# Second graph layer's score stage: TensorE runs 22 of its 25 tile groups in an engine loop of 11 turns

## The chip, the cores and the metric

The kernel runs on one core of one Trainium2 chip. The metric is the device time of one execution in microseconds (us), lower is better. "TensorE" is PE in the profile (its weight loads are PEld), "VectorE" is DVE, "ScalarE" is ACT, "GpSimd" is POOL, and the queue that only issues DMAs is SP.

## The reference, cut to what matters

The model is four graph layers, each followed by a feed-forward layer, on 384 nodes of 512 features with 12288 edges. The change lies in the third graph layer by position, called L2 in the code (the second layer of the kind that scatters messages along sorted edges, counting from L0). What it computes:

```python
h_src = h[src]                                   # rows of h = x @ W.T, 8 heads of 64
e_src = einsum('ehd,hd->eh', h_src, a_src)
e_dst = einsum('ehd,hd->eh', h[dst], a_dst)
e = leaky_relu(e_src + e_dst, 0.2) * (1 + et_emb[edge_type]) * edge_weight[:, None]
e_max = zeros((n, h_)).at[dst].max(e)
e = exp(e - e_max[dst]);  e_sum = zeros((n, h_)).at[dst].add(e)
alpha = e / (e_sum[dst] + 1e-10)
out = zeros(...).at[dst].add(h_src * alpha[:, :, None])
```

The score stage is the sum `e_src + e_dst` for every edge and head. Everything from `leaky_relu` on needs it.

## The kernel before

Edges lie sorted by destination in 98 tiles of 128 (`TT2 = 98`), worked in groups of four (`GT = 4`), so 25 groups (`GG`), the last of two tiles. One group passes through four steps on three engines:

- **Key rows** (TensorE, `key_row`, L2481): for each of two keys (source node, destination node within its chunk of 128), four matmuls spread a column of key values, broadcast as weights, over a bank of PSUM. Two banks, jobs `l2b{g}0` and `l2b{g}1`, eight matmuls of 128 columns in 16-bit float.
- **Copy** (ScalarE, L2551): each bank goes to SBUF as `key_rows`, 128x512.
- **Compare** (VectorE, L2659): four comparisons with the node number give `node_hot`, one-hot matrices, and the semaphore `nodes_ready` counts the group.
- **Score** (TensorE, L2496 to L2505): per tile four matmuls of 24 columns into one bank, job `l2e{g}`. Three have fixed operands, the fourth reads `dst_parts` at a place that comes from a register (`four[j]`). The registers are loaded from a list in SBUF, four tiles at once, by `chunks_of` (L678). VectorE then sums the bank to `w_edge` (`score`, L2650), one group behind its comparisons.

TensorE's program is written out: key rows of group g+2, then the wait for `nodes_ready` of group g, then the scores of group g. PSUM has eight banks, handed out in turn by `Banks.open` (L54), so a bank comes back after 8 jobs, that is after 2.7 groups. Each bank has two semaphores, "full" (counted up by TensorE's last matmul of the job) and "free" (counted up by its reader). `Banks.loop` (L66) exists for TensorE loops elsewhere in the kernel, and waits inside such a loop compare with a value that depends on the turn's number.

At the same time GpSimd gathers rows of `tab_h` with indirect DMAs (`pool_scatter_rows`, L633): one DMA for each of the 98 tiles, in series of six, with a wait for their landing between. There are 39 places for rows, so DMA 39 waits until the scatter stage has used the first. Ahead of the 13th and the 20th DMA (`POOLED_SCORES`) GpSimd waits for the scores of groups 0 to 8 and 9 to 15, and scales them with four operations each (L2587 to L2590). The rest is scaled by VectorE at L2669 and L2672, then the maxima are formed (L2677 to L2700), and the scatter stage begins (`pe_scatter_rows`, L694): for each tile one matmul of 128x512 float32 on the gathered row and one of 24 columns.

The first graph layer has a TensorE loop of 13 turns of 8 tiles (L958), all of whose large matmuls take an operand at a place from a register. It serves as a measure of such operands.

Of the kernel before, what the change touches and what calls it, by code (L numbers as in the profile page):

```python
# [162 lines left out]
def gnn_ffn_program(nc, A, out):  # L163
    ctx = ExitStack()
    with ctx:
# [511 lines left out]

        def chunks_of(T):  # L678
            _, some = nc.values_load_multi_w_load_instructions(
                chunk2_i[0:1, T:min(T + 4, TT2)], engines=[mybir.EngineType.PE], min_val=0, max_val=NT - 1,  # L680
                skip_runtime_bounds_check_because="a sum of two comparisons is 0, 1 or 2")
            return some

# [1751 lines left out]
        POOLED_SCORES = {12: (0, 9), 19: (9, 16)}  # L2435
        SCORED_LATE = GT * 16

        w_here = {}

        def along(v):  # L2440
# [14 lines left out]
        @on("pe")  # L2455
        def _(pe, o):
            pe.wait_ge(tiles_loaded, 16)
            b = banks.open(pe, "l2n")
            nc.tensor.transpose(b[0:TT2, 0:P], dst2, ident[:])
            for s_, lane in enumerate((0, P - 1)):  # L2460
                last = mm(b[0:H8, P + s_ * TT2:P + (s_ + 1) * TT2], ident[:, lane:lane + 1].broadcast_to([P, H8]), dst2, True, True)
            last.then_inc(banks.full_of("l2n"), 1)
            wT = ring.get(pe, 0)
            w_here["L2"] = 16 * ring.got[0]
            ends = banks.open(pe, "l2a_")
            for t in range(NT):
                for k in ((0,), (1, 2), ())[t]:
                    pe_turn_block(pe, "l2x", xn, k, 3 * NT)
                if t == 0:
                    pe.wait_ge(cols_ready, 1)  # L2470
                banks.drained(pe, f"l2x{t}")
                b = banks.open(pe, f"l2r{t}")
                for c in range(KC):
                    own = xT[:, c, t * P:(t + 1) * P]
                    last = mm(b, own, wT[:, c, :], c == 0, c == KC - 1)
                    if c == KC - 1:
                        last.then_inc(banks.full_of(f"l2r{t}"), 1)
                    last = mm(ends[:, t * 2 * H8:(t + 1) * 2 * H8], own, fold[:, c, :], c == 0, c == KC - 1)
            last.then_inc(banks.full_of("l2a_"), 1)

            def key_row(g):  # L2481
                for f in range(2):
                    b = banks.open(pe, f"l2b{g}{f}")
                    for j in range(min(GT, TT2 - GT * g)):
                        last = mm(b[:, j * P:(j + 1) * P], key_cols[:, f, GT * g + j:GT * g + j + 1].broadcast_to([P, P]), ident_h,
                                  True, True)
                    last.then_inc(banks.full_of(f"l2b{g}{f}"), 1)

            pe.wait_ge(cols_ready, 2)
            key_row(0)  # L2490
            key_row(1)
            pe.wait_ge(step_ready, 6)
            for g in range(GG):
                if g + 2 < GG:
                    key_row(g + 2)
                pe.wait_ge(nodes_ready, g + 1)  # L2496
                b = banks.open(pe, f"l2e{g}")
                four = chunks_of(GT * g)
                for j in range(min(GT, TT2 - GT * g)):
                    o = b[:, j * 3 * H8:(j + 1) * 3 * H8]  # L2500
                    for c in range(NT):
                        mm(o, node_hot[:, g % 2, c, j * P:(j + 1) * P], parts[:, 0, c, :, :].rearrange("p k h -> p (k h)"),
                           c == 0, False)
                    last = mm(o, node_hot[:, g % 2, NT, j * P:(j + 1) * P], dst_parts[:, bass.ds(four[j] * 3 * H8, 3 * H8)], False, True)
                last.then_inc(banks.full_of(f"l2e{g}"), 1)  # L2505

            pe.wait_ge(lanes_ready, 1)
            banks.at = SUMS + 1
            for k in range(2):
                b = banks.open(pe, f"l2t{k}")  # L2510
                for h in range(HH):
                    last = nc.tensor.transpose(b[0:TT2, h * P:(h + 1) * P], w_edge[:, :, HH * k + h], ident[:])
                last.then_inc(banks.full_of(f"l2t{k}"), 1)
            pe_clear_sums(pe, "l2")
            banks.at = SUMS + 3
            pe.wait_ge(lanes_ready, 2)
            b = banks.open(pe, "l2m")
            mm(b[0:H8, 0:TT2], weight[:, :, 0], ident[0:TT2, 0:TT2], True, True)
            mm(b[0:H8, TT2:2 * TT2], top[:, :, P - 1], ident[0:TT2, 0:TT2], True, True).then_inc(banks.full_of("l2m"), 1)
            pe.wait_ge(lanes_ready, 3)  # L2520
            b = banks.open(pe, "l2w")
            for s_ in range(2):
                last = mm(b[0:TT2, s_ * H8:(s_ + 1) * H8], lane_fwd[:, :, s_], ident[0:H8, 0:H8], True, True)
            last.then_inc(banks.full_of("l2w"), 1)
            banks.at = SUMS + 3
            for k in range(2):
                pe.wait_ge(lanes_ready, 4 + k)
                b = banks.open(pe, f"l2v{k}")
                for h in range(HH):
                    last = nc.tensor.transpose(b[:, h * TT2:(h + 1) * TT2], weight[:, HH * k + h, :], ident[0:TT2, 0:TT2])  # L2530
                last.then_inc(banks.full_of(f"l2v{k}"), 1)
            pe_scatter_rows(pe, "l2")

        @on("act")
        def _(act, o):

            act_row_std(act, ROW_L2, 0)
            act_turned_block(act, "l2x", xT, 0)
            for t in range(1, NT):
                act_row_std(act, ROW_L2 + t, t)  # L2540
            for t in range(1, NT):
                act_turned_block(act, "l2x", xT, t)
            for t in range(NT):
                act_copy(act, f"l2r{t}", hrows[:, t, :])
            for g in range(GG):
                if g >= 2:
                    act.wait_ge(nodes_ready, g - 1)
                for f in range(2):
                    b = banks.filled(act, f"l2b{g}{f}")
                    n = P * min(GT, TT2 - GT * g)  # L2550
                    nc.scalar.activation(key_rows[:, g % 2, f, 0:n], b[:, 0:n], ACT.Copy).then_inc(banks.free_of(f"l2b{g}{f}"), 1)  # L2551
            act_hot_half(act, 0)
            for k in range(2):
                b = banks.filled(act, f"l2v{k}")
                nc.scalar.activation(w_tile[:, HH * k:HH * k + HH, :].rearrange("p h t -> p (h t)"), b[:, 0:HH * TT2],
                                     ACT.Exp).then_inc(banks.free_of(f"l2v{k}"), 1)
            for i in range(1, TT2 // RB):
                act_hot_half(act, i)
            banks.drained(act, "l2s")
            for t in range(1, NT):  # L2560
                b = banks.filled(act, f"l2a{t}")
                for h in range(H8):
                    last = nc.scalar.activation(xn2[:, t, h * HD:(h + 1) * HD], b[:, h * HD:(h + 1) * HD], ACT.Identity,
                                                scale=gate[:, 4, t * H8 + h:t * H8 + h + 1])
                last.then_inc(banks.free_of(f"l2a{t}"), 1)
                if t == 1:
                    act_row_std(act, ROW_F2, 0)
            act_row_std(act, ROW_F2 + 1, 0)
            for t in range(1, NT):
                act_row_std(act, ROW_F2 + 2 * t, t)  # L2570
                act_turned_block(act, "f2x", xT, t - 1)
                act_row_std(act, ROW_F2 + 2 * t + 1, t)
            act_turned_block(act, "f2x", xT, NT - 1)

        @on("pool")
        def _(pool, op):
# [3 lines left out]
            def between(T):  # L2580
                if T not in POOLED_SCORES:
                    return
                g0, g1 = POOLED_SCORES[T]
                banks.all_drained(pool, [f"l2e{g}" for g in range(g0, g1)])
                own = slice(GT * g0, GT * g1)
                small = sel8[:, own, :]
                op.link(nc.gpsimd.tensor_scalar(small, w_edge[:, own, :], 0.0, 0.2, ALU.min, ALU.mult))  # L2587
# [48 lines left out]
        def _(dve, od):  # L2636
# [8 lines left out]
            nc.vector.memset(gate[:, 15, 5:6], 0.0).then_inc(step_ready, 1)  # L2645

            def score(g):
                b = banks.filled(dve, f"l2e{g}")
                n = min(GT, TT2 - GT * g)
                nc.vector.tensor_reduce(w_edge[:, GT * g:GT * g + n, :],  # L2650
                                        b[:, 0:n * 3 * H8].rearrange("p (t k h) -> p t h k", t=n, k=3), AX,
                                        ALU.add).then_inc(banks.free_of(f"l2e{g}"), 1)

            for g in range(GG):
                n = P * min(GT, TT2 - GT * g)
                for f in range(2):
                    banks.drained(dve, f"l2b{g}{f}")
                    for c in range(NT) if f == 0 else (0,):
                        last = nc.vector.tensor_scalar(node_hot[:, g % 2, c + NT * f, 0:n], key_rows[:, g % 2, f, 0:n],  # L2659
                                                       node_id[:, c:c + 1], None, ALU.is_equal)  # L2660
# [1 line left out]
                if g >= 1:  # L2662
                    score(g - 1)
            score(GG - 1)
            banks.all_drained(dve, [f"l2e{g}" for g in range(GG)])

            late = slice(SCORED_LATE, TT2)
            dve.wait_ge(factor_ready, 1)
# [624 lines left out]
```

## Time and profile before

| | us |
|---|---|
| median of 3 runs | 1792.34 (1790.09 to 1795.05) |
| profiled execution | 1795.19 |
| its span, first to last instruction | 1793.4 |
| PE busy | 1601.0 (89%) |
| DVE busy | 881.6 (49%) |
| ACT busy | 501.5 (28%) |
| POOL busy | 642.0 (36%) |

The profile's times are counted from the start of the span. Waits that the trace can't connect with an instruction's end are marked "remote": the semaphore moved, but no instruction that counts it up ended shortly before. "issue" is time in which an engine waited for nothing that the profile shows. PEclk is the share of full clock that TensorE was granted. Register operations, branches and waits of the sequencers are not among the rows.

### The profile page before, as it was taken

The numbers are of one execution on the slowest core, as the hardware profiler recorded it, in microseconds if no ns is written. First come the engines' busy times: TensorE is split into PE (matmuls) and PEld (weight loads), VectorE is DVE, ScalarE is ACT, GpSimd is POOL, SyncE is SP. The second block draws the span as 40 slices with busy tenths as digits, with TensorE's granted clock in tenths as the row PEclk, the third lists the DMA queues.
The fourth block names the chain that finished last, engine by engine and source line by source line (L and its number), as shares of the span: only waits on it lengthen the run. The fifth ranks groups of instructions, "written<-read, shape, count | busy, mean of one in ns | idle before, by whom it ended". The sixth has DMA issues, their size and how long they took to land. (4 is left out here: it accounts for less than half of the span.)

```text
span 1793.4 us, 22802 instructions
## 1 busy us (share of the span) xinstructions
PE 1601.0 (89%) x6910; PEld 888.4 (50%) x6940; DVE 881.6 (49%) x2161; ACT 501.5 (28%) x1586; POOL 642.0 (36%) x756
## 2 busy tenths in 40 slices
PE   6989999998697999999996877589799999999798
PEld 3534444446444645555553645334344555555555
DVE  8878888878644343344354154598623101111322
ACT  1134444447431413223231124311200111111234
POOL 5868787873332333333341713556300000000000
PEclk9989999999698999999997887589799999999899
DMA  8030101005413223122316744445326121220020
GB/s 313 2 102 25 60 25 60 25 8 133 124 48 127 78 82 90 57 81 63 94 42 135 255 138 140 138 133 160 118 71 216 51 91 52 99 67 16 9 62 18
DMA packets 119611, 161.71 MB, mean 90 GB/s; under 512 B 49497, under 2 KB 61721, under 8 KB 119154
## 3 DMA queue, kind: packets, MB, share of 16 engines
q1 hardware_dynamic: 93056, 115.43, 20.6%
q0 software_dynamic: 18592, 29.91, 6.1%
q10 hardware_dynamic: 7890, 15.44, 2.6%
q8 instruction: 41, 0.67, 0.2%
q14 instruction: 32, 0.26, 0.1%
HBM read 145.26 MB, written 15.47 MB: 90 GB/s over the span
## 5 line engine op out<-in xcount | busy, mean ns | idle before, releaser
L373 PE MATMUL psum<-arena 128*128 128x384 f32 (+9 forms) x1804 | 319.8, 333 | 33.0 <-issue 13.3
L373 PE MATMUL psum<-arena,ring 128*128 (+1 forms) x1478 | 323.2, 364 | 9.0 <-issue 6.3
L373 PE MATMUL psum<-xT,ring 128*128 128x384 f32 x928 | 317.5, 503 | 10.4 <-ACT ring L3118 4.5
L373 PEld LDWEIGHTS psum<-arena 128*128 128x128 f32 (+5 forms) x1804 | 197.3, 155 | 162.8 <-issue 88.3
L373 PE MATMUL psum<-ring,arena 128*128 128x512 f32 (+1 forms) x570 | 261.9, 607 | 8.6 <-DVE ring L663 3.9
L373 PE MATMUL psum<-ring,xT 128*128 128x512 f32 x552 | 253.9, 613 | 2.1 <-DMA bc<-in_wide 0.8
L373 PEld LDWEIGHTS psum<-xT,ring 128*128 128x128 f32 x928 | 181.5, 197 | 139.9 <-issue 28.3
L373 PEld LDWEIGHTS psum<-arena,ring 128*128 128x128 bf16 (+1 forms) x1504 | 139.7, 115 | 130.3 <-issue 29.0
L1071 ACT ACTIVATE ring<-ring 128x128 f32<-128x128 f32 x416 | 123.3, 297 | 173.6 <-DVE ring L1357 164.6
L373 PEld LDWEIGHTS psum<-ring,xT 128*128 128x128 f32 x552 | 106.0, 197 | 125.4 <-issue 121.6
L373 PEld LDWEIGHTS psum<-ring,arena 128*128 128x128 f32 (+1 forms) x570 | 99.7, 188 | 131.3 <-issue 130.2
L851 POOL DMA_INDIRECT tab_bucketed<-rec,pos x96 | 95.7, 997 | 190.0 <-DMA tab_bucketed<-rec,pos 182.4
L2144 POOL DMA_INDIRECT tab_sorted<-rec,pos x104 | 100.0, 962 | 173.2 <-DMA tab_sorted<-rec,pos 151.1
L1357 DVE SCALAR_TENSOR_TENSOR ring<-psum,wa 128x1024 f32<-128x1024 f32 x104 | 127.3, 1224 | 61.4 <-PE psum L373 60.5
L1165 POOL TENSOR_SCALAR arena<-iota,arena 128x128 bf16<-128x128 f32 x200 | 121.6, 616 | 16.8 <-DVE xT L1371 13.9
L1177 POOL DMA_INDIRECT tab_w<-xT,pair x104 | 109.8, 1056 | 48.8 <-DMA tab_w<-xT,pair 31.9
L408 ACT ACTIVATE arena<-psum 128x384 f32<-128x384 f32 (+1 forms) x130 | 61.9, 498 | 182.8 <-PE psum L373 157.6
L482 ACT ACTIVATE std<-mv,eps_col 128x1 f32<-128x1 f32 x57 | 16.8, 294 | 220.9 <-DVE mv L465 217.9
L1071 ACT ACTIVATION_READ_ACCUMULATOR ring<-ring 128x1 f32 x416 | 77.5, 186 | 0.0
L624 POOL DMA_INDIRECT ring<-tab_h,sd_t x61 | 62.6, 1026 | 37.1 <-issue 13.3
L2071 DVE TENSOR_TENSOR xn<-xn,psum 128x512 f32<-128x512 f32 x24 | 16.5, 687 | 118.7 <-PE psum L373 118.5
L1365 DVE TENSOR_REDUCE mask_dst<-ring 128x4 f32<-128x512 f32 x104 | 70.2, 675 | 0.0
(478 smaller groups left out, 1667.3 us busy)
## 6 DMA issues: line engine op xcount, KB each, us to landing
ring<-in_L_ffn_w SPq DMA_DIRECT2D x22, 1024.0 KB, 6.8
ring<-in_L_gnn_m_w SPq DMA_DIRECT2D x8, 1024.0 KB, 6.0
ring<-in_L_ffn_expert_weights SPq DMA_DIRECT2D x8, 1024.0 KB
ring<-tab_key ACTq DMA_DIRECT2D x24, 256.0 KB
ring<-in_L_gnn_Wv SPq DMA_DIRECT2D x5, 1024.0 KB, 5.1
tab_w<-xn SPq DMA_DIRECT2D x6, 768.0 KB, 14.7
ring<-in_L_gnn_Ww SPq DMA_DIRECT2D x4, 1024.0 KB
ring<-in_L_gnn_wq SPq DMA_DIRECT2D x4, 1024.0 KB
```

Source lines behind the costliest of these rows:

```text
L373: return nc.tensor.matmul(o, a, b, start=start, stop=stop)
L408: nc.scalar.activation(dst, b[:, 0:w], ACT.Copy).then_inc(banks.free_of(name), 1)
L482: nc.scalar.activation(std[:, t:t + 1], mv[:, t, 1:2], ACT.Sqrt, bias=eps_col[:, 0:1]).then_inc(row_std, 1)
L624: return nc.gpsimd.indirect_dma_start(o, None, table, bass.IndirectOffsetOnAxis(ap=column.bitcast(U32), axis=0), **more)
L851: nc.gpsimd.indirect_dma_start(tab_bucketed, bass.IndirectOffsetOnAxis(ap=pos[:, q:q + 1].bitcast(U32), axis=0), rec[:, q, :], None).then_ ...
L1071: last = nc.scalar.activation(prod2[:, b % 2, h, :], prod2[:, b % 2, h, :], ACT.Copy, accum_out=w_sum[:, b, h:h + 1])
L1165: last = nc.gpsimd.tensor_scalar(edge_is[:, j, k, s_, :], iota[:, 0:P], key_rq[:, s_, T:T + 1], None, ALU.is_equal)
L1177: nc.gpsimd.indirect_dma_start(tab_w, bass.IndirectOffsetOnAxis(ap=pair[:, q:q + 1].bitcast(U32), axis=0), w_edge0[:, q, :], None).then_in ...
L1357: V.scalar_tensor_tensor(out=prod2[:, b % 2], in0=z_bank[:, b % 2], scalar=0.0, in1=wa_all, op0=ALU.max, op1=ALU.mult).then_inc(z_free, 1)
L1365: V.tensor_reduce(w_sum[:, b, 0:H8 // 2], prod2[:, b % 2, 0:H8 // 2, :], AX, ALU.add).then_inc(halves_summed, 1)
L2071: V.tensor_tensor(xn2[:, t, :], xn2[:, t, :], b, ALU.add).then_inc(banks.free_of(f"{tag}{t}"), 1)
L2144: nc.gpsimd.indirect_dma_start(tab_sorted, bass.IndirectOffsetOnAxis(ap=pos2[:, q:q + 1].bitcast(U32), axis=0), rec[:, q, :], None).then_i ...
```

## The change

Key rows and scores of a group become functions that take either fixed numbers or a place that depends on the loop's register. Groups 0 to 21 run in an engine loop of TensorE, 11 turns of two groups; groups 22 to 24 stay written out. In the loop the column of key values, the place in the list of chunks, and the values that the waits compare with all come from the turn's register. The loop uses six banks, the same ones in every turn, so a bank comes back after two groups. The other engines stay written out, and their waits name the same banks by the new jobs. GpSimd and VectorE wait for the last two or five groups' banks rather than for one job of each bank.

```diff
         def chunks_of(T):
             _, some = nc.values_load_multi_w_load_instructions(
-                chunk2_i[0:1, T:min(T + 4, TT2)], engines=[mybir.EngineType.PE], min_val=0, max_val=NT - 1,
+                chunk2_i[0:1, slice(T, min(T + 4, TT2)) if isinstance(T, int) else bass.ds(T, 4)], engines=[mybir.EngineType.PE], min_val=0, max_val=NT - 1,
...
+        TURNS = (GG - 3) // 2
+        def key_job(g, f):
+            return (f"l2b{g % 2}{f}_", (g - 2) // 2) if 2 <= g < 2 * TURNS + 2 else (f"l2b{g}{f}", None)
+
+        def score_job(g):
+            return (f"l2e{g % 2}_", g // 2) if g < 2 * TURNS else (f"l2e{g}", None)
...
-            def key_row(g):
+            def key_row(g, tiles=GT, at=None, i=None):
                 for f in range(2):
+                    job = key_job(g, f)[0]
+                    b = banks.open(pe, job, i)
+                    for j in range(tiles):
+                        col = key_cols[:, f, GT * g + j:GT * g + j + 1] if at is None else key_cols[:, f, bass.ds(at + j, 1)]
+                        last = mm(b[:, j * P:(j + 1) * P], col.broadcast_to([P, P]), ident_h, True, True)
+                    last.then_inc(banks.full_of(job), 1)
+
+            def scored(g, tiles=GT, at=None, i=None):
+                job = score_job(g)[0]
+                pe.wait_ge(nodes_ready, g + 1 if i is None else 2 * i + g + 1)
+                b = banks.open(pe, job, i)
+                four = chunks_of(GT * g if at is None else at)
+                for j in range(tiles):
                     o = b[:, j * 3 * H8:(j + 1) * 3 * H8]
                     for c in range(NT):
                         mm(o, node_hot[:, g % 2, c, j * P:(j + 1) * P], parts[:, 0, c, :, :].rearrange("p k h -> p (k h)"),
                            c == 0, False)
                     last = mm(o, node_hot[:, g % 2, NT, j * P:(j + 1) * P], dst_parts[:, bass.ds(four[j] * 3 * H8, 3 * H8)], False, True)
-                last.then_inc(banks.full_of(f"l2e{g}"), 1)
+                last.then_inc(banks.full_of(job), 1)
+
+            pe.wait_ge(cols_ready, 2)
+            key_row(0)
+            key_row(1)
+            pe.wait_ge(step_ready, 6)
+            with banks.loop(TURNS, 6, first=banks.at), pe.Fori(0, TURNS) as i:
+                for h in range(2):
+                    key_row(2 + h, at=2 * GT * i + GT * (2 + h), i=i)
+                    scored(h, at=2 * GT * i + GT * h, i=i)
+            for g in range(2 * TURNS, GG):
+                if g + 2 < GG:
+                    key_row(g + 2, min(GT, TT2 - GT * (g + 2)))
+                scored(g, min(GT, TT2 - GT * g))
...
-                banks.all_drained(pool, [f"l2e{g}" for g in range(g0, g1)])
+                for g in (g1 - 2, g1 - 1):
+                    banks.drained(pool, *score_job(g))
...
-            banks.all_drained(dve, [f"l2e{g}" for g in range(GG)])
+            for g in range(2 * TURNS - 2, GG):
+                banks.drained(dve, *score_job(g))
```

## Rows read from the trace of the kernel before

**Rows 1.** Page: busy us of each engine (share of the span) xinstructions.

```profile
PE 1601.0 (89%) x6910; PEld 888.4 (50%) x6940; DVE 881.6 (49%) x2161; ACT 501.5 (28%) x1586; POOL 642.0 (36%) x756
```

**Rows 2.** Chain that ended last, in order of time: start us, us, what.

```profile
1154.37 0.46 DVE arena L2669
...
1173.43 0.51 ACT arena L2555
1174.02 0.70 DVE arena L663
1174.96 54.40 PE psum L373 x159
...
1272.27 4.14 DMA ring<-tab_h,sd_t
```

**Rows 3.** Waits, 1092.3 to 1154: waiter <- waited for: us, times, longest.

```profile
DVE arena L2650 <- remote: 24.2, 6, 5.3
ACT arena L2551 <- remote: 18.4, 7, 4.6
PE psum L373 <- DVE arena L2659: 12.6, 11, 3.1
```

**Rows 4.** Timeline of VectorE: start us, us, engine line op, count, [idle before <-releaser].

```profile
1093.22 0.26 DVE L2650 TENSOR_REDUCE arena<-psum 128x32 f32<-128x96 f32 x1 [0.72 <-PE psum L373]
1097.20 1.13 DVE L2659 TENSOR_SCALAR arena<-arena,node_id 128x512 bf16<-128x512 f16 x4
...
1127.14 0.26 DVE L2650 TENSOR_REDUCE arena<-psum 128x32 f32<-128x96 f32 x1 [5.32 <-remote]
1128.36 0.25 DVE L2650 TENSOR_REDUCE arena<-psum 128x32 f32<-128x96 f32 x1
1129.69 0.26 DVE L2650 TENSOR_REDUCE arena<-psum 128x32 f32<-128x96 f32 x1
...
1145.08 0.26 DVE L2650 TENSOR_REDUCE arena<-psum 128x32 f32<-128x96 f32 x1
1149.25 0.26 DVE L2650 TENSOR_REDUCE arena<-psum 128x32 f32<-128x96 f32 x1 [2.73 <-remote]
1153.61 0.37 DVE L2650 TENSOR_REDUCE arena<-psum 128x32 f32<-128x96 f32 x2 [3.33 <-remote]
```

**Rows 5.** Timeline, 1109 to 1116, TensorE, ScalarE and VectorE.

```profile
1111.07 0.50 PE L373 MATMUL psum<-arena 128*128 128x24 bf16 x5 [0.51 <-DVE arena L2659]
1111.40 0.60 ACT L2551 ACTIVATE arena<-psum 128x512 f16<-128x512 f32 x1 [2.98 <-remote]
1112.78 0.18 PE L373 MATMUL psum<-arena 128*128 128x24 bf16 x1 [1.21 <-issue]
1113.50 0.18 PE L373 MATMUL psum<-arena 128*128 128x24 bf16 x1 [0.54 <-issue]
1115.77 0.26 DVE L2650 TENSOR_REDUCE arena<-psum 128x32 f32<-128x96 f32 x1 [5.13 <-remote]
```

**Rows 6.** Stretches: us, PE, PEld, DVE, ACT, POOL busy (x), PEclk, DMA share, GB/s.

```profile
1130.00:1135.00 5.00, 4.63 (x79) 4.30 (x78) 4.94 (x16) 3.77 (x7) 3.77 (x5) 0.51 0.19 56
1138.00:1142.50 4.50, 1.98 (x20) 1.12 (x20) 0.00 (x0) 0.64 (x2) 2.79 (x3) 0.53 0.71 195
1096.40:1096.83 0.43, 0.43 (x18) 0.43 (x16) 0.00 (x0) 0.00 (x0) 0.43 (x1) 0.50 0.97 338
198.53:221.44 22.91, 22.25 (x135) 10.93 (x136) 18.48 (x52) 10.22 (x65) 16.15 (x22) 1.00 0.28 93
```

**Rows 7.** Timeline of TensorE: three runs of matmuls in the stage.

```profile
1090.46 0.62 PE L373 MATMUL psum<-arena 128*128 128x128 f16 x8 [0.43 <-DVE gate L2645]
...
1098.76 0.40 PE L373 MATMUL psum<-arena 128*128 128x24 bf16 x7 [1.09 <-DVE arena L2659]
...
1146.94 0.84 PE L373 MATMUL psum<-arena 128*128 128x24 bf16 x16 [0.67 <-DVE arena L2659]
```

**Rows 8.** First layer's loop, one such matmul per tile: min/median/max ns, first and last start.

```profile
L373 PE MATMUL psum<-ones_b,arena x104: 167/167/211, 106.8 to 403.2; 128*128 128x1 bf16 x104
```

**Rows 9.** DMA queues, 1087 to 1155: packets, MB, share of 16 engines.

```profile
q0 software_dynamic: 2400, 7.87, 38.9%
q1 hardware_dynamic: 1472, 2.90, 12.4%
q8 instruction: 5, 0.08, 0.4%
```

**Rows 10.** Waits of GpSimd, 1155 to 1178, and its timeline around its first scaling.

```profile
POOL arena L624 <- PE psum L373: 7.6, 1, 7.6
...
1113.32 0.94 POOL L624 DMA_INDIRECT ring<-tab_h,sd_t  x1 [0.30 <-issue]
1114.29 1.23 POOL L2587 TENSOR_SCALAR arena<-arena 128x288 f32<-128x288 f32 x1
```

More of the change, by code:

```diff
@@ L2436, in gnn_ffn_program @@
         SCORED_LATE = GT * 16
+        TURNS = (GG - 3) // 2
+        assert 2 * TURNS + 3 == GG
+        def key_job(g, f):
+            return (f"l2b{g % 2}{f}_", (g - 2) // 2) if 2 <= g < 2 * TURNS + 2 else (f"l2b{g}{f}", None)
+        def score_job(g):
+            return (f"l2e{g % 2}_", g // 2) if g < 2 * TURNS else (f"l2e{g}", None)
         w_here = {}
@@ L2479, in _ @@
             last.then_inc(banks.full_of("l2a_"), 1)
-            def key_row(g):
+            def key_row(g, tiles=GT, at=None, i=None):
                 for f in range(2):
[L2483 to L2499, printed above, removed]
+                    job = key_job(g, f)[0]
[10 more added lines that the diff above has]
+                for j in range(tiles):
                     o = b[:, j * 3 * H8:(j + 1) * 3 * H8]
@@ L2548, in _ @@
                 for f in range(2):
-                    b = banks.filled(act, f"l2b{g}{f}")
+                    b = banks.filled(act, *key_job(g, f))
                     n = P * min(GT, TT2 - GT * g)
-                    nc.scalar.activation(key_rows[:, g % 2, f, 0:n], b[:, 0:n], ACT.Copy).then_inc(banks.free_of(f"l2b{g}{f}"), 1)
+                    nc.scalar.activation(key_rows[:, g % 2, f, 0:n], b[:, 0:n], ACT.Copy).then_inc(
+                        banks.free_of(key_job(g, f)[0]), 1)
             act_hot_half(act, 0)
@@ L2647, in score @@
             def score(g):
-                b = banks.filled(dve, f"l2e{g}")
+                b = banks.filled(dve, *score_job(g))
                 n = min(GT, TT2 - GT * g)
@@ L2651, in score @@
                                         b[:, 0:n * 3 * H8].rearrange("p (t k h) -> p t h k", t=n, k=3), AX,
-                                        ALU.add).then_inc(banks.free_of(f"l2e{g}"), 1)
+                                        ALU.add).then_inc(banks.free_of(score_job(g)[0]), 1)
             for g in range(GG):
@@ L2656, in _ @@
                 for f in range(2):
-                    banks.drained(dve, f"l2b{g}{f}")
+                    banks.drained(dve, *key_job(g, f))
                     for c in range(NT) if f == 0 else (0,):
```

## The prediction

> **What bounds the kernel now.** I read the page first: TensorE is busy 89% of the span [rows 1], but that is an average, and the question is what ends the score stage and what its end moves. The chain of waits after the stage runs without a gap from VectorE's L2669 at 1154.37 through the maxima to the scatter stage, which starts at 1174.02 and in which TensorE holds the chain for 54.4 us at a stretch [rows 2]. So a score stage that ends later moves all that follows by the same time. An earlier end is worth less: GpSimd's DMA 39 waited 7.6 us for the scatter stage [rows 10], and the chain ends the scatter stage on the landing of the last gathered row, 4.14 us [rows 2]. Once the gain passes about 8 us, the gathers set the pace and the rest of it is lost.
>
> Next the stage itself, by waits and timeline. VectorE sums group 0 at 1093.22 and group 21 at 1145.08: 21 steps in 51.86 us, 2.47 us a group; the last three groups follow by 1153.98 [rows 4]. But the three steps from 1127.14 to 1129.69 are 1.22 and 1.33 us [rows 4]. The difference is in six waits of VectorE marked "remote", 24.2 us together, and seven of ScalarE, 18.4 us [rows 3]. In such a wait TensorE's matmuls had long been recorded, yet their semaphores did not move. At 1111.07 five matmuls go out, then one at 1112.78 and one at 1113.50, and the sum that VectorE waits for starts only at 1115.77 [rows 5]. From 1130 to 1135 TensorE does 79 matmuls; from 1138 to 1142.5 it does 20, while the DMA share goes from 0.19 to 0.71 [rows 6]. These **stops** fall into the series of gathers, which are the stage's largest traffic (2400 packets, 7.87 MB) [rows 9]. What they are the trace does not say. What matters here is that the stage is paced by two things, the clear pace of about 1.3 us a group, and the stops.
>
> **The change part by part.** What is taken away: TensorE's code for 20 of 22 groups need not be loaded. The stage loads five blocks of code [rows 9]. I cost this at nothing, and the rival below tells what it would be worth if that is wrong. Matmuls, copies, comparisons and sums are the same in number and size. The transfers that GpSimd and SP issue are the same too, and SP is not moved past anything.
>
> What is added is work of TensorE's sequencer, and no row shows such work by itself, so I bound it.
>
> (a) *An operand from a register.* A group's 16 score matmuls, four of them with one, take 0.84 us less the last one's own 0.18, so 0.66 us [rows 7], where TensorE with work in hand does 18 in 0.43 us, 0.024 us each [rows 6]. Four such operands so cost between (0.66 - 16 x 0.024)/4 = 0.07 us, if the plain matmuls count fully, and 0.66/4 = 0.165 us, if they hide. The first layer's loop gives the same upper end: 104 tiles from 106.8 to 403.2 us are 2.88 us a tile [rows 8] with 17 such matmuls, 0.17 us each, but there TensorE is busy for 22.25 of 22.91 us [rows 6], so it hides some. I take 0.12, the middle, as both rows bear on it.
>
> (b) *Key rows.* Eight matmuls with fixed operands take 0.62 us less 0.22 for the last, 0.057 us each [rows 7]. With an operand from a register each they take 8 x 0.12 = 0.96 us of the sequencer (0.56 to 1.36).
>
> (c) *Start of the scores.* From the end of the comparisons at 1097.20 + 1.13 = 1098.33 [rows 4] to the first score matmul at 1098.76 [rows 7] are 0.43 us: the wait, and the load of the four registers. The place in the list is now computed, one more of (a): 0.12.
>
> (d) *Waits with a value from the register.* Four a group (two key banks, `nodes_ready`, one score bank). No row has one alone; between nothing and the price of an address, so 0 to 0.66 a group. I take 0.24, half of four times 0.12, since in (a) the address is the nearest thing.
>
> (e) *The turn's end.* The first layer's loop idles 0.66 us in a whole turn [rows 6], so at most 0.66, at least nothing, per turn of two groups here; I take 0.15 a group.
>
> A group in the loop: 0.43 + 0.12 + 0.66 + 0.96 + 0.24 + 0.15 = **2.56 us**; with all the low ends 0.43 + 0.07 + 0.66 + 0.56 = 1.72, with all the high ones 0.43 + 0.17 + 0.66 + 1.36 + 0.66 + 0.33 = 3.61. VectorE's 1.3 us no longer paces the stage in clear stretches; TensorE's sequencer does. The edit is not hidden: the cover it has is the 1.3 us pace and the waits of TensorE for the comparisons, 12.6 us over the stage [rows 3], and 22 x (2.56 - 1.3) = 28 us is more than that. What is queued behind TensorE's waits are its own next key rows, and ScalarE and VectorE wait for those.
>
> Six banks rather than eight: a key bank is wanted back after two groups. ScalarE's copy of it was made before the comparisons that TensorE has by then waited for, so this costs nothing at 2.56 us a group.
>
> Without any stop 21 steps take 21 x 2.56 = 53.8 us, against 51.86 now: **+1.9 us**. Of the stops now, 24.2 - 2.73 - 3.33 = 18.1 us lie in these 21 steps [rows 3, 4]. How much stays is the hard step. If TensorE does nothing in a stop, all stays: +1.9 + 18.1 = +20. If the stops come only of the dense stream of matmuls, none stays: +1.9. What speaks for between: in a stop TensorE still did 20 matmuls in 4.5 us [rows 6], and a slower stream takes longer to run into one. At 24 matmuls per 2.56 us it would want 42 in that time. I take that 60% stays, 0.6 x 18.1 = 10.9, so **+13 us**. The last three groups are as before.
>
> GpSimd waits for group 8 ahead of its 13th DMA. Now it needn't (1113.32 + 0.94, then L2587 at 1114.29 [rows 10]); then group 8 comes some 5 us later and the gathers slip with it, also ahead of the 20th. DMA 39 waited 7.6 us, and the scatter stage slips by 13 us itself, so this stays covered; without that cover it would add its own 5 to 10 us.
>
> The profiled execution took 1795.19, so profiled 1808; the median of the runs is 2.85 below it, so **1792.3 + 13 = 1805 us**.
>
> **What the Trainium skill says against this change.** In the first layer's loop, whose turn holds 135 matmuls and 136 weight loads, TensorE is idle for 0.66 us in a whole turn [rows 6]. The Trainium skill, "Runtime: NRT & Kernel Launch", section "Instruction fetch mechanics", says that code is streamed in blocks of 256 instructions, mostly hidden, and that a taken branch to a block outside the two-block window stalls until it is fetched. By it a turn's end could stall here, if the turn lies across a block's edge; by the row it does not, for a longer turn, and the sum takes (e) from the row. The same section's "mostly hidden" is also against the second rival below.
>
> **The rivals.**
>
> *The stops go away altogether.* For it: the first layer's loop has a thinner stream (135 matmuls in 22.91 us, 6 per us against 16 per us from 1130 to 1135 [rows 6]) and is almost gapless with other indirect DMAs beside it. The loop here would have 9 per us. Against: TensorE was thin in the stops too. It gives +2, less up to 6 if the three last groups lose their stops (2.73 + 3.33 [rows 4]): 1788 to 1798, likeliest 1794, so "same".
>
> *The stops are code loading, and it is faster.* For it: five blocks [rows 9] and about five stops. Against: matmuls already recorded got their semaphores late [rows 5], which code that is not there yet can't do. If so, all 18.1 us of stops go, and with operands at the low end (1.72 us a group, 36 us for 21 steps) the stage ends 16 us earlier; at the middle price it is no gain, so this decides only below 2.2 us a group. Of the 16, some 8 pass the gathers: 1784.
>
> *The stops take the added instructions too.* If a stop holds back every instruction of the sequencer, address work included, then there are a third more of them and the stops grow: 24 instead of 18.1 us, and with 2.7 us a group rather than 2.56, since the waits of (d) then cost nearer their high end, 57 + 24 - 52 = +29: 1821.
>
> *The change doesn't do what it says,* as when the stage's end is set elsewhere: 1792.
>
> **How the numbers follow.** My forecast, slower by 6 to 20 us: 0.47. The added instructions in the stops: 0.15. Stops gone: 0.22 (of it 0.17 same, 0.03 slower, 0.02 faster). Code loading: 0.13 (0.11 faster, 0.02 same). No effect: 0.03, same. About 0.3%, 5.4 us, is what a measurement here can tell from no change. Slower 0.65, same 0.22, faster 0.13. The range runs from 1788, the low end of the gone stops, to 1823, above the forecast with whole stops (+20) and the third rival's 1821; outside are the code loading case and the high ends of all prices.
>
> **What would show it.** Right: VectorE's steps from sum to sum in clear stretches go from 1.3 to about 2.6 us; "remote" waits of VectorE fall to about 10 us; VectorE's wait for TensorE at L2650 rises well over the few us it has now; L2669 starts at about 1167. Blocks of code in the stage fall from five to two or so. Operands too dear or cheap: clear steps of 3 or 2 us. Stops gone: no "remote" wait left. Code loading: the stops end with the blocks. The forecast is wrong in sign if clear steps are below 2.2 us and the stops are gone.

## The result, and the profile after

The changed kernel takes 1794.37 us (median of 20 runs, 1791.01 to 1798.76) against 1790.67 us before (20 runs, 1788.29 to 1795.05): ratio 1.0020, 95% interval 1.0013 to 1.0027. So it is slower, by 3.7 us, which is less than the 0.3% that I had called "same". I forecast 1805, +13. The profiled execution took 1795.85 us, with a span of 1794.0, against 1795.19 and 1793.4.

Page after: busy us of each engine, then the queue that loads code (41 packets in the whole execution before).

```profile
PE 1609.5 (90%) x6910; PEld 892.3 (50%) x6940; DVE 882.3 (49%) x2161; ACT 502.1 (28%) x1586; POOL 644.9 (36%) x756
...
q8 instruction: 37, 0.61, 0.1%
```

Waits after, 1092.3 to 1154, answering [rows 3]: waiter <- waited for: us, times, longest.

```profile
ACT arena L2569 <- PE psum L373: 33.5, 22, 1.9
DVE arena L2670 <- PE psum L373: 26.6, 24, 1.7
```

Timeline of VectorE after, answering [rows 4].

```profile
1094.88 0.26 DVE L2670 TENSOR_REDUCE arena<-psum 128x32 f32<-128x96 f32 x1 [1.23 <-PE psum L373]
...
1150.22 0.26 DVE L2670 TENSOR_REDUCE arena<-psum 128x32 f32<-128x96 f32 x1 [0.99 <-PE psum L373]
...
1154.00 0.21 DVE L2670 TENSOR_REDUCE arena<-psum 128x16 f32<-128x48 f32 x1 [0.76 <-PE psum L373]
1154.44 0.44 DVE L2690 SCALAR_TENSOR_TENSOR arena<-arena 128x272 f32<-128x272 f32 x1 [0.24 <-DVE arena L2670]
```

Stretches after, answering [rows 6]: us, busy (x) of PE, PEld, DVE, ACT, POOL, PEclk, DMA share, GB/s.

```profile
1130.00:1135.00 5.00, 3.68 (x48) 2.82 (x46) 2.45 (x10) 2.26 (x4) 1.09 (x2) 0.50 0.22 64
1138.00:1142.50 4.50, 3.25 (x44) 2.46 (x43) 2.51 (x9) 2.21 (x4) 3.44 (x5) 0.50 0.41 114
```

No wait is marked "remote". The 21 steps from the sum of group 0 to that of group 21 take 55.34 us, 2.64 us a group. TensorE does the same 10 matmuls per us whether the gathers run or not, and the stage ends where it ended before: 1154.44 against 1154.37 [rows 2]. Read alone, this pair of traces says that the loop cost 28 us (55.3 less 21 x 1.3) and that the stops, which went away, gave as much back. That reading is wrong. The experiments show that the pair compares an execution with stops to one without, and that the change isn't what takes them away.

### The profile page after: what moved, and what is told of

Same layout as the page of the kernel before. It is cut to its first block, busy times and chain, and to the rows that moved or that the text cites. A ratio compares the mean times of both kernels' runs of the same rounds, so it can differ in the third digit from the quotient of the medians.

```text
span 1794.0 us, 23093 instructions
## 1 busy us (share of the span) xinstructions
PE 1609.5 (90%) x6910; PEld 892.3 (50%) x6940; DVE 882.3 (49%) x2161; ACT 502.1 (28%) x1586; POOL 644.9 (36%) x756
## 4 chain that ended last, share of the span: by engine, by line
PE 83%; DVE 10%; issue 3%; ACT 2%; DMA 1%; POOL 1%; ACTq 0%; DVEq 0%; another core or an unknown queue 0%; POOLq 0%
PE psum L373 81%; DVE stats L464 1%; DVE arena L2679 1%; DVE ring L1291 1%; PE psum L1020 1%; DVE xn L2052 0%; DMA ring<-tab_h,sd_t 0%; DVE xn L2058 0%; DVE xn L2071 0%; DVE mv L465 0%; DMA arena<-tab_x 0%; PE psum L2281 0%; ACT xT L408 0%; DMA x<-in_x 0%; POOL tab_x L2324 0%
## 5 line engine op out<-in xcount | busy, mean ns | idle before, releaser
L373 PE MATMUL psum<-arena 128*128 128x384 f32 (+9 forms) x1804 | 329.4, 333 | 25.3 <-issue 12.5
L373 PEld LDWEIGHTS psum<-arena 128*128 128x128 f32 (+6 forms) x1804 | 201.9, 153 | 159.5 <-issue 81.8
L373 PEld LDWEIGHTS psum<-xT,ring 128*128 128x128 f32 x928 | 181.6, 197 | 139.8 <-issue 28.5
```

Of the source, the lines that this page charges most:

```text
L373: return nc.tensor.matmul(o, a, b, start=start, stop=stop)
```

## The experiments

The kernels ran in six groups, A to F. The kernels of one group ran on one chip and are compared with runs of the kernel before on that same chip; the record numbers the chips 1 (A), 0 (B), 1 (C), 10 (D), 5 (E) and 15 (F). "Remote waits" and "length" come from the one profiled execution of each kernel. "Length" is from the start of the sum of group 0 to that of the last group, 24 steps.

| group, median before | run | ratio (95%) | remote waits of VectorE, us | length, us |
|---|---|---|---|---|
| A 1798.88 | e1_written_out | 1.0001 (0.9992 to 1.0010) | 23.7 | 60.6 |
| A | e2_loop_dense | 1.0013 (1.0003 to 1.0024) | 27.0 | 63.7 |
| A | e3_gathers_held | 1.0089 (1.0073 to 1.0105) | none | 30.7 |
| B 1794.06 | e4_registers_unrolled | 1.0042 (1.0028 to 1.0057) | 23.5 | 65.6 |
| B | e5_half_the_registers | 1.0034 (1.0019 to 1.0048) | 24.5 | 61.7 |
| B | e6_loop_gathers_held | 1.0273 (1.0256 to 1.0290) | none | 59.0 |
| B | e7_slow_vector | 1.0124 (1.0107 to 1.0141) | 5.2 | 75.5 |
| C 1789.74 | e8_registers_more | 0.9998 (0.9988 to 1.0009) | none | 53.2 |
| C | e9_registers_all | 1.0020 (1.0010 to 1.0030) | none | 54.3 |
| C | e10_loop_half | 0.9991 (0.9979 to 1.0003) | none | 49.9 |
| D 1790.44 | e11_before_again | 0.9994 (0.9985 to 1.0004) | none | 34.2 |
| D | e12_after_again | 1.0018 (1.0008 to 1.0028) | none | 59.1 |
| D | e13_registers_again | 1.0000 (0.9989 to 1.0011) | none | 52.7 |
| D | e14_half_again | 0.9987 (0.9975 to 0.9998) | none | 49.9 |
| E 1797.60 | e15_before_third | 1.0007 (0.9986 to 1.0028) | 25.4 | 60.1 |
| E | e16_after_third | 1.0053 (1.0039 to 1.0068) | 28.5 | 72.6 |
| F 1797.19 | e17_half_third | 1.0043 (1.0029 to 1.0056) | 28.3 | 66.9 |

### Group A: what makes the stops?

My theory after the result (A): a dense stream of TensorE while the gathers run makes the stops, and the loop's thin stream does not. The rival (B): the loading of code makes them.

**e1_written_out.** The groups are written out in a loop of one turn, for operands from a register without a short loop.

```
-            for g in range(GG):
+            with banks.loop(1, 6 * TURNS, first=at0), pe.Fori(0, 1) as i:
+                for g in range(2 * TURNS):
+                    key_row(g + 2, at=i + GT * (g + 2), i=i)
+                    scored(g, at=i + GT * g, i=i)
```

> Groups 0 to 21 are written out as before, so all their code is loaded, but the column of each key matmul and the values of the waits come from a register (a loop of one turn around all 22 groups). This has the thin stream of the changed kernel (2.64 us a group) with the code loading of the kernel before. Theory A, the stops come from the dense stream of matmuls while gathers run: no remote wait of VectorE in the stage, the last sum at 1154 us as in the changed kernel, time 0 to +4 us against before. Theory B, the stops come from code loading while gathers run: four or five remote waits of 2 to 5 us stay, the last sum at 1165 to 1175, time +12 to +25 us against before.

Its clear steps are 1.22 us, so the register price was not there: it is in effect the kernel before again, with the same time, and tells the theories apart in nothing.

**e2_loop_dense.** The loop; ScalarE copies the key columns of a group to a fixed place.

```
+                    pe.wait_ge(cols_staged, 2 * i + h + 1)
...
-                        col = key_cols[:, f, GT * g + j:GT * g + j + 1] if at is None else key_cols[:, f, bass.ds(at + j, 1)]
+                        col = key_cols[:, f, GT * g + j:GT * g + j + 1] if at is None else key_now[:, g % 2, f, j:j + 1]
```

> The loop of the changed kernel, but ScalarE copies the four key columns of each group to a fixed place (one small operation more a group), so that the eight key matmuls take no operand from a register. By the changed kernel's steps a group should cost TensorE 2.64 - 8 x 0.07 to 0.12 = 1.7 to 2.1 us. Theory A (dense stream): stops come back, at least 10 us of remote waits of VectorE, the last sum at 1145 to 1155, time within 4 us of before. Theory B (code loading): no stop, the last sum at 1092 + 22 x 1.9 + 4 = 1138, and the time is 6 to 10 us below before and 9 to 13 us below the changed kernel, less than the stage gains, since the gathers then set the pace.

**e3_gathers_held.** The kernel before, with GpSimd waiting for the last comparison ahead of its gathers.

```
+            pool.wait_ge(nodes_ready, GG)
```

> The kernel before, but GpSimd starts its gathers only after the comparisons of all 25 groups. Both theories expect no stop if the gathers are needed for one: 25 groups at 1.3 to 1.5 us, the last sum at 1092 + 36 = 1128. If code loading alone or the dense stream alone makes the stops, remote waits of over 10 us stay and the last sum comes after 1140. The time tells what the gathers' head start is worth: 39 rows at about 1.9 us then start at 1128 rather than at 1095, so +25 to +40 us against before.

Waits of VectorE, 1085 to 1175, of e2_loop_dense, then of e3_gathers_held:

```profile
DVE arena L2682 <- remote: 27.0, 8, 6.3
```

```profile
DVE arena L2673 <- POOL arena L2591: 35.8, 1, 35.8
...
DVE arena L2651 <- PE psum L373: 1.6, 3, 0.8
```

In e2 the stops are there though only one block of code is loaded in the stage; in e3 five blocks are loaded (1097.7, 1102.5, 1107.5, 1114.6, 1121.5) and there is no stop: 1.28 us a group, the whole stage in 30.7 us. This refutes theory B, and shows that in this group there are stops only with gathers beside (one profiled execution each). By the same page as in the prediction, the Trainium skill, "Runtime: NRT & Kernel Launch", section "Instruction fetch mechanics", code loading is mostly hidden; e3 agrees, with 1.28 us a group through five blocks. I took e2 for a proof of theory A too. It wasn't one, since no kernel with a thin stream and gathers was in the group.

### Groups B and C: is it the rate?

**e4_registers_unrolled.** As e1 was meant: a register loaded from memory, which holds 0.

```
+            zero = nc.values_load(nought[0:1, 0:1], engines=[mybir.EngineType.PE], min_val=0, max_val=1,
...
-  key_cols[:, f, GT * g + j:GT * g + j + 1]
+  key_cols[:, f, bass.ds(zero + T, 1)]
```

> The kernel before, written out for all 25 groups, no loop; but TensorE's key rows of groups 2 to 23 and the place of the load of the four chunk registers are addressed with a register that was loaded from memory and holds 0, so the compiler cannot fold it away. The first experiment was meant to do this and did not: its clear steps were 1.22 us. Theory A (stops come of a dense stream of TensorE while the gathers run): steps of about 2.3 us a group (the loop's 2.64 less its turn's end of about 0.25 a group and less register waits), no remote waits, with all five blocks of code loaded as before; last sum near 1148 to 1153, time within 5 us of the kernel before. Theory B' (it is the loop itself, its short code or its two semaphore counts, that keeps the stops away): stops stay, 15 to 20 us of remote waits on top of the 2.3 us steps, last sum past 1160, 8 to 15 us slower than before.

**e5_half_the_registers.** The same for `f == 0` only, with the chunk load as before.

> As e4_registers_unrolled, but only the first of a group's two key rows is addressed with the register (4 of 8 key matmuls), and the chunk load is as before. Steps of about 1.7 to 1.9 us a group by the sum of the prediction. Theory A with a smooth dependence: some stops stay, remote waits of VectorE of 5 to 15 us, and the last sum again near 1150. Theory A with a threshold between 16 and 9 matmuls per us that this stream (13 per us) is below: no stops, last sum near 1136 to 1140, and up to about 8 us faster than before, where the gathers set the pace.

**e6_loop_gathers_held.** The changed kernel with the wait of e3.

> The changed kernel, with GpSimd held back from its gathers until all comparisons of the stage are done. It prices the loop by itself. If no part of the 2.64 us a group in the changed kernel is a stop: the same steps of 2.6 us, 21 steps 55 us, last sum near 1153, and the scatter stage late by the whole of the gathers' delay, about 20 to 25 us slower than the kernel with the gathers held and all groups written out (1815.7). If half or more of the 2.64 us were stops in disguise, the steps fall towards 2 us, 21 steps near 42 to 45 us.

**e7_slow_vector.** Four more comparisons a group on VectorE, result unread.

```
+                    for _ in range(4 * f):
+                        od.link(nc.vector.tensor_scalar(dull_rows[:, 0:n], key_rows[:, g % 2, 0, 0:n],
+                                                               node_id[:, 0:1], None, ALU.is_equal))
```

> The kernel before, but VectorE makes four more comparisons a group into a buffer of its own that nobody reads (about 1.2 us a group), so TensorE has the same instructions with fixed operands and the same dense bursts of 24 matmuls, but waits in between, about 2.5 us a group on average. If the stops depend on the mean rate of TensorE over a group, they are gone: no remote waits, steps of 2.5 us, last sum near 1152 to 1155, time about that of the kernel before plus 0 to 5 us. If they depend on the burst, so on how closely one matmul follows the next, they stay or shrink little: remote waits of VectorE above 10 us, last sum past 1162, 8 to 20 us slower than before.

e4 has the thin stream and six blocks of code, and 23.5 us of remote waits; e5, with five blocks, has 24.5. Theory A in its simple form fell here. e6 takes 55.4 us for the 21 steps, the changed kernel 55.3 with its gathers beside, so nothing in 2.64 us is a stop in disguise. e6 against e3 also gives the loop's price without any cover: 28.3 us of length. In time it is 27.4 us by the medians (1843.05 and 1815.65), or some 33 us by the ratios (1.0273 and 1.0089), since the two ran in different groups. e7 kept smaller stops (5.2 us for VectorE, 9.0 for ScalarE) at 2.8 us a group, but GpSimd waited 15.3 us for the sums in its two places, which held up the gathers. How much of its 22.5 us comes of that and how much of the longer stage is not separated, so e7 decides nothing.

**e8_registers_more**, **e9_registers_all.** As e4, with one, then all of a tile's score matmuls addressed by the register too. **e10_loop_half.** e2 with only the second key row from the fixed place.

```
+                        own = node_hot[:, g % 2, c, j * P:(j + 1) * P]
+                        if g < GG - 3 and c in (0,):
+                            own = node_flat[:, bass.ds(zero + (g % 2 * (NT + 1) + c) * GT * P + j * P, P)]
```

> As e4_registers_unrolled (written out, no loop), with four more register operands a group: the first of each tile's four score matmuls. By the sum, clear steps near 2.6 to 2.7 us, as in the changed kernel, at the same 9 matmuls per us and evenly spread. Theory R (what keeps the stops away is an even stream of at most some 9.6 matmuls per us, made by the sequencer's own work): no remote waits or nearly none, last sum near 1154 to 1157, with five or six blocks of code loaded. Theory L (something of the loop keeps them away): remote waits of VectorE above 15 us on top of the steps, last sum past 1163.

> As e8_registers_more, but all sixteen score matmuls and all eight key matmuls of a group take a register operand: clear steps near 3.6 us, 7 matmuls per us. Theory R: no remote waits, 21 steps of 3.6 us, last sum near 1175, some 20 us slower than before. Theory L: remote waits on top, last sum past 1185. It stands beside the one before in case the bound lies a little lower than 9.6.

> The loop, with the first key row from a register operand and the second from the fixed place into which ScalarE copies: between the changed kernel (eight register operands in the key rows, no stops) and e2_loop_dense (none, stops). Clear steps near 2.1 us, 11 to 12 matmuls per us, with one block of code in the stage. Theory R with the bound between 9.6 and 12: stops come back, remote waits of VectorE of 10 us or more. Theory L or a bound above 12: no remote waits, last sum near 1143, up to 8 us faster than before.

A stretch of e4_registers_unrolled (group B), then the same of e8_registers_more (group C):

```profile
1110.00:1115.00 5.00, 1.87 (x20) 1.17 (x17) 1.48 (x7) 1.23 (x3) 1.85 (x2) 0.50 0.62 184
```

```profile
1110.00:1115.00 5.00, 4.01 (x51) 3.26 (x51) 3.32 (x12) 2.51 (x6) 4.01 (x4) 0.50 0.71 208
```

The added operands of e8 and e9 turned out to cost nothing: e8 takes 2.35 us a group, e9 2.33 after its first, and e4 2.2 to 2.35 where it is clear. So e4 and e8 have one stream, and one has stops and the other none. The rate doesn't tell them apart; what does was another thing, and the groups were the nearest: all of B without held gathers had stops, all of C none. Neither group has a profile of the kernel before.

### Groups D, E and F: the same kernels on other chips

e11 and e15 are the kernel before, e12 and e16 the changed one, e13 is e4, e14 and e17 are e10, each without an edit.

> The kernel before, unchanged, for a second profile on the chip of this call. e4_registers_unrolled had stops and e8_registers_more had none, yet their streams are the same where both are clear: 2.33 us a group in both, with the same instructions apart. They ran on different chips. Theory R (the rate decides): the stops are here again, 20 to 25 us of remote waits of VectorE, last sum near 1150, whatever the chip. Theory C (the stops belong to a chip, or to an execution, and not to the kernel): it may have none; then the last sum is near 1125 and what sets the end is the gathers and TensorE in the scatter stage.

> The changed kernel, unchanged, beside the one before it on the same chip. Theory R: no remote waits, steps of 2.64 us, last sum near 1154, and the time 3 to 4 us over the kernel before. Theory C: remote waits of some 20 us if e11_before_again has them, last sum past 1160; if that has none, this has none either, and the last sum is some 28 us later than that kernel's.

> e4_registers_unrolled once more. It had 23.5 us of remote waits. Theory C: stops if and only if e11_before_again has them, without them 2.33 us a group, last sum near 1149, and the ratio to the kernel before near 1.000 as for e8_registers_more, not 1.004. Theory R: stops again, ratio near 1.004, also if e11_before_again were free of them.

> e10_loop_half once more, the only version so far whose median was below the kernel before (0.9991). Theory R: no remote waits, last sum near 1140, ratio 0.998 to 1.000 and below the changed kernel's by 3 us or more. Theory C: with stops if this chip has them, and then a ratio of 1.001 or more, as e2_loop_dense had.

> The kernel before once more, in hope of a chip or an execution with stops: e11_before_again had none, the recorded profile had 24.2 us of remote waits of VectorE. If it has them: last sum near 1150. If not: near 1127, GpSimd's factors again the last thing that VectorE waits for.

> The changed kernel beside it. If e15_before_third has stops: with theory D (stops belong to chip or execution and take any kernel's stream) this has them too, last sum past 1160, 5 us or more slower than before on this chip; with theory R' (even where the chip has stops, this stream escapes them) none, last sum near 1152. If e15_before_third has none, this has none, and the question stays open.

> e10_loop_half once more, on whatever chip comes. On a chip where the kernel before has a median near 1798 (as with e15_before_third, which had stops): stops here too, since the stops went with the chip in all sixteen kernels; a group takes 2.2 us rather than 2.64, so 21 steps are 9 us shorter than the changed kernel's before the stops, and the ratio lies between e2_loop_dense (1.0013) and e16_after_third (1.0053), about 1.003. On a chip near 1790: no stops, ratio 0.998 to 1.000, as twice before.

The kernel before, 1120 to 1125, in group D (e11), then in group E (e15):

```profile
1120.00:1125.00 5.00, 4.40 (x81) 4.01 (x80) 4.98 (x20) 3.24 (x7) 3.78 (x5) 0.50 0.64 170
```

```profile
1120.00:1125.00 5.00, 1.82 (x14) 0.97 (x13) 0.94 (x4) 1.14 (x3) 2.20 (x3) 0.50 0.69 201
```

Same kernel, same gathers, DMA share 0.64 and 0.69, same granted clock: 81 matmuls and 14. Nor is it the traffic as such. At the stage's start, in the same execution of e15, the DMA engines are full with other transfers (no row of a gather moves yet), and TensorE does 93 matmuls:

```profile
1090.00:1095.00 5.00, 5.00 (x93) 4.79 (x91) 3.18 (x13) 2.17 (x4) 2.17 (x3) 0.66 1.02 344
```

Waits of e15_before_third, then of e16_after_third, 1085 to 1170:

```profile
DVE arena L2650 <- remote: 25.4, 7, 5.3
...
ACT arena L2551 <- remote: 20.1, 7, 5.6
```

```profile
DVE arena L2670 <- remote: 28.5, 6, 6.2
...
ACT arena L2569 <- remote: 23.6, 6, 6.2
```

Timeline of VectorE in e16_after_third: a stop, the backlog after it, and the stage's end.

```profile
1094.81 0.26 DVE L2670 TENSOR_REDUCE arena<-psum 128x32 f32<-128x96 f32 x1 [1.16 <-PE psum L373]
...
1102.30 0.26 DVE L2670 TENSOR_REDUCE arena<-psum 128x32 f32<-128x96 f32 x1 [6.19 <-remote]
...
1103.52 0.25 DVE L2670 TENSOR_REDUCE arena<-psum 128x32 f32<-128x96 f32 x1
...
1165.40 0.45 DVE L2690 SCALAR_TENSOR_TENSOR arena<-arena 128x272 f32<-128x272 f32 x1 [0.24 <-DVE arena L2670]
```

So the stops go with the chip or with its condition at the time. In A, B, E and F every profiled kernel whose gathers run beside the scores has them; in C and D none has, in D the kernel before included. Groups A and C bear the same chip number, 1, and A has stops while C has none. If the number names the same chip both times, which the record doesn't say, then it is the condition and not the chip. Every kernel that ran in both sorts shows it: the kernel before, the changed one, the registers written out (e4, e13) and the half loop (e10 and e14, e17).

The runs that were not profiled bear this out. The mean granted clock of a whole execution is on record for each run of the kernel before: in C and D it is 0.936 to 0.945 in all 66, in A, B, E and F 0.930 to 0.939 in all 67. The times part in the same way, with medians of 1789.74 to 1790.44 in C and D and of 1794.06 to 1798.88 in the others. So a group as a whole is of one sort, and not only its profiled executions.

Where there are **no stops** (D), the stage is 24.9 us longer with the loop, 59.1 against 34.2, and the median only 2.95 us longer (1792.86 against 1789.91). VectorE after its last sum, e11_before_again, then e12_after_again:

```profile
1127.64 0.44 DVE L2669 SCALAR_TENSOR_TENSOR arena<-arena 128x272 f32<-128x272 f32 x1 [0.39 <-DVE arena L2650]
1134.32 0.44 DVE L2672 TENSOR_TENSOR arena<-arena 128x272 f32<-128x272 f32 x1 [6.24 <-POOL arena L2590]
```

```profile
1149.65 0.51 DVE L2690 SCALAR_TENSOR_TENSOR arena<-arena 128x272 f32<-128x272 f32 x1 [0.24 <-DVE arena L2670]
1150.19 0.44 DVE L2693 TENSOR_TENSOR arena<-arena 128x272 f32<-128x272 f32 x1
```

Chain of e11_before_again, then of e12_after_again, through the scatter stage: start us, us, what.

```profile
1154.46 65.24 PE psum L373 x195
1219.89 1.17 POOL xT L624
...
1267.61 4.25 DMA ring<-tab_h,sd_t
```

```profile
1170.30 86.24 PE psum L373 x258
1256.91 0.96 POOL ring L624
...
1269.91 3.83 DMA ring<-tab_h,sd_t
```

The kernel before ends its stage early and then waits 6.24 us for GpSimd's scaling of the scores, which stands behind GpSimd's 19th gather. What is left of its lead at the scatter stage, 15.8 us (1170.30 - 1154.46), TensorE loses again in the scatter stage: it holds the chain for 65.24 us and then waits for gathers, while in the changed kernel it holds it for 86.24. The last gather's landing starts 2.3 us apart, the spans are 0.3 us apart. In both the last gathers stand at the end of the chain.

Where there **are stops** (E), that cover is used up. GpSimd's gathers are held up too: from 1090 to 1150 it waits 9.9 us for VectorE's sums in e16 and 4.5 in e15. The stage is 12.5 us longer (72.6 - 60.1), L2690 comes at 1165.40 where e15 has L2669 at 1151.25, and the spans are 11.5 us apart (1805.1 and 1793.6), the medians 10.5 (1808.60 and 1798.06).

e10, e14 and e17 are the version that looked best, 0.1% faster than the kernel before in D. In F, where there are stops, it is 0.4% slower (1.0043). No version here is faster than the kernel before on both sorts of chip.

## Why the prediction was wrong

**The step that failed** is the one called hard, "of the stops now ... 60% stays, 0.6 x 18.1 = 10.9", and what is wrong in it is not the share but the premise that the stops belong to the kernel and are there in the runs compared. With it fails a second step, "a score stage that ends later moves all that follows by the same time": in D, without stops, the stage is 24.9 us longer and the median only 2.95 us. Where there are stops I can put the same numbers side by side. The 21 steps take 51.5 us in e15 and 30.5 in e11: the stops cost the kernel before 21.0 us, where I had taken 18.1. They take 68.4 in e16 and 55.3 in e12: 13.1 us in the changed kernel, 62% of it. The forecast there was 53.8 + 10.9 = 64.7 us, the stage's end near 1167 (1165.40 measured) and +13 (+11.5 measured). My own three signs, "remote" waits down to about 10, L2669 near 1167, slower by 13, gave one miss in that group, since 28.5 us of remote waits are all still there; a smaller part of each is lost, because in a stop the thin stream falls less behind (steps of 1.22 us after most stops catch up).

But the 20 runs of the result have 1.0020, like D with 1.0018 and unlike E with 1.0053, so most of them were probably without stops; the single profile that I argued from, 4.5 us above the median of its kernel, was not. What else there is points the same way: the changed kernel's 20 runs take at most 1798.76 us, where e16's seven take 1806.03 or more, and 15 of them have a granted clock above 0.930, where none of e16's has. Still it is argued, not shown, since only profiled executions show stops, and the clocks of the kernel before are not on record for these runs. I had seen that the profiled execution lay above the median of three and had only subtracted it.

**The prices were right.** (a) to (e) summed to 2.56 us a group; it is 2.64. The half loop, with four operands from a register fewer and one wait more, takes 2.20: 0.11 us each, against 0.12 taken. Written out it is 2.33 (e13), so (d) and (e) are 0.30 together, against 0.39 taken. But the price is not one of any such operand: the 4 and 12 that e8 and e9 add to the score matmuls cost nothing (2.35 and 2.33 us a group). Their places recur in every second group, those of the key rows are new in each. Whether that is the reason was not tested. (A slip in the reading: the sums from 1127.14 to 1129.69 are three, so the steps of 1.22 and 1.33 us are two.)

**The last three groups "as before"**: 3.8 us after (1154.00 - 1150.22) against 8.7 before, and 4.2 us in e16. A slip, since I had myself said that 6 us of these were stops.

**The cover.** "An earlier end is worth less" was right, and larger than I made it. I said that past 8 us a gain is lost; from the stops' side, the kernel before is already beyond this point where it has none, and then the loop's 25 us land in that same cover. I had put the gathers down as a cap on a gain and never asked what the kernel before would look like without stops, though I gave the change a rival without them. DMA 39's wait, called covered, was: it waits 7.3 us for TensorE in e15 and 10.2 in e16, where the scatter stage comes later.

```profile
1174.23 1.14 POOL L624 DMA_INDIRECT arena<-tab_h,sd_t  x1 [7.28 <-PE psum L373]
```

```profile
1188.36 1.14 POOL L624 DMA_INDIRECT arena<-tab_h,sd_t  x1 [10.18 <-PE psum L373]
```

**The rivals.** "The stops go away altogether" gave 1794, and 1794.37 was measured; the trace after looks just like it. Its mechanism is still refuted: the changed kernel has stops in E. It was right in time by luck: it took a kernel before with stops, 1.9 us of loop and the end of the last stops, where without stops the loop lengthens the stage by 24.9 us and nearly all of it is covered behind the gathers. "Code loading" is refuted by e2 and e3. "The stops take the added instructions too" (1821) is refuted by e16: the stops cost 13.1 us, not 24.

## What to carry to other kernels

If one profile shows waits that no instruction explains, look in a second execution, on another chip or at another time, before you build on them: an effect that comes and goes without the kernel makes a before and an after look like a cause and its cure. Profile both kernels in one group. Ask what the kernel looks like with the effect and without it, and put the change's price against the slack of each; here the loop cost 3 us where there were no stops and 11 where there were. In this loop on TensorE an address from the turn's register cost 0.11 us for each key matmul. VectorE's 1.3 us a group was too short to hide eight of them; what hid them, where there were no stops, was the slack behind the stage.

## What the runs showed of the hardware

The stops: while GpSimd's gathers move up to 200 GB/s, TensorE's stream falls from 81 to 14 matmuls in 5 us and VectorE waits up to 6 us for matmuls that are long on record. In two groups they are absent under the same traffic, and with the gathers held back (e3, e6) they are absent in groups that have them. At a DMA share of 1.02 from other transfers TensorE did 93 matmuls in 5 us (e15, 1090 to 1095). What the stops are is open.

TensorE's granted clock was 1.00 (2.4 GHz) from 1100 to 1115 in e11, with some 91 matmuls per 5 us, and 0.50 (1.2 GHz) in the same stretch of e12 with 48; e11, then e12:

```profile
1100.00:1105.00 5.00, 4.68 (x92) 4.01 (x92) 4.96 (x19) 4.06 (x8) 2.04 (x2) 1.00 0.58 177
```

```profile
1100.00:1105.00 5.00, 3.97 (x48) 2.98 (x47) 2.65 (x10) 1.82 (x5) 1.86 (x2) 0.50 0.33 80
```

The full clock was of little use to e11, whose VectorE is busy for 4.96 of the 5 us: its steps are 1.24 to 1.63 us from 1100 to 1115, and 1.23 to 1.44 from 1120 on, where the clock is 0.50. What the low one costs the loop, with steps of 2.3 and 3.0 us by turns, isn't shown, since no run has the loop at full clock.
